# Soft combine on one NeuronCore: the maxima move from a TensorE product to a VectorE subtraction, the 1/Z weighing moves to GpSimd

## The reference

```python
def _L1_ffn_ref(x, phi_w, phi_b, expert_w, expert_b):
    logits = (jnp.einsum('tzd,ed->tze', x, phi_w) + phi_b).reshape(t, z, n, p)   # 64 experts x 32 slots
    D = jax.nn.softmax(logits, axis=3)
    C = jax.nn.softmax(logits, axis=2)
    X_tilde = jnp.einsum('tznp,tzd->npd', D, x)
    ...
    Y_tilde = jnp.einsum('npd,ndH->npH', X_tilde, expert_w) + expert_b[:, None, :]
    return jnp.einsum('tznp,npH->tzH', C, Y_tilde)
x = x + 0.5 * _L1_ffn_ref(_layernorm(x), ...)
```

## Time and profile before

| What | Value |
|---|---|
| median of 3 runs | 2346.54 us (2342.49 to 2348.29) |
| the profiled execution, its time | 2333.07 us |
| the profiled execution, its span | 2331.2 us |
| mean granted TensorE clock | 0.943 of full |
| combine of the first soft stage | about 1332 to 1606 us of the span |
| combine of the second soft stage | about 2056 to 2331 us, the end of the program |

### The profile page before, as it was taken

How to read it: one execution, slowest core, us unless ns; L and a number is a source line. 1 busy time by engine, 2 the same in 40 slices (tenths; PEclk the granted TensorE clock), 3 DMA queues, 4 the chain that set the end, 5 groups by cost and what they waited for, 6 DMA issues and landing times.

```text
span 2331.2 us, 23318 instructions
## 1 busy us (share of the span) xinstructions
PE 1947.9 (84%) x6378; PEld 958.2 (41%) x6400; DVE 1627.1 (70%) x2176; ACT 1034.7 (44%) x1548; POOL 1230.9 (53%) x775
## 2 busy tenths in 40 slices
PE   4099576888888717968999899997977999999998
PEld 3077422333333505753444344443333444444443
DVE  7133587999999822348999666674895999856554
ACT  2322286555555232225555453342444555463332
POOL 4645104999999473526999500001973999900000
PEclk9999796999999958989999999998988999999999
DMA  7122383555555022323000000002633000000000
GB/s 256 56 87 89 100 131 108 177 172 174 176 169 179 32 70 77 106 91 91 0 0 0 0 1 0 0 0 71 170 94 90 0 0 0 0 1 10 4 9 14
DMA packets 108594, 163.42 MB, mean 70 GB/s; under 512 B 11379, under 2 KB 74174, under 8 KB 108391
## 3 DMA queue, kind: packets, MB, share of 16 engines
q1 hardware_dynamic: 100326, 146.23, 21.5%
q0 software_dynamic: 8192, 16.30, 2.1%
HBM read 124.89 MB, written 38.15 MB: 70 GB/s over the span
## 4 chain that ended last, share of the span: by engine, by line
PE 53%; DVE 17%; issue 14%; POOL 11%; ACT 4%; DMA 1%; POOLq 0%; DVEq 0%; ACTq 0%; SPq 0%
PE ps L1904 10%; PE ps L1877 10%; PE ps L1636 5%; POOL arena L560 5%; PE ps L1833 5%; PE ps L1823 5%; PE ps L1646 5%; PE ps L1762 3%; DVE arena L1331 2%; POOL slot_inputs L506 2%; PE ps L1878 2%; POOL arena L539 1%; DVE arena L1497 1%; DVE stats L1055 1%; DVE stage L1080 1%
## 5 line engine op out<-in xcount | busy, mean ns | idle before, releaser
L568 POOL TENSOR_TENSOR arena<-arena 128x1024 f32<-128x1024 f32 x128 | 244.7, 1912 | 79.5 <-DVE arena L1384 74.0
L1823 PE MATMUL ps<-c_phiT,arena 128*128 128x512 f32 x512 | 266.8, 603 | 8.4 <-ACT arena L809 5.3
L1877 PE MATMUL ps<-XT,c_phiT 128*128 (+1 forms) x512 | 261.9, 593 | 0.9
L1833 PE MATMUL ps<-arena 128*128 128x512 f32 x512 | 241.2, 595 | 5.6 <-POOL arena L560 5.6
L560 POOL TENSOR_TENSOR arena<-arena 128x1024 f32<-128x1024 f32 x128 | 244.7, 1913 | 0.0
L534 POOL TENSOR_TENSOR arena<-XT,arena 128x1024 f32<-128x1024 f32 x86 | 170.0, 2000 | 140.3 <-DMA arena<-input_gates 140.3
L1904 PE MATMUL ps<-arena 128*128 128x512 f32 x512 | 226.2, 601 | 11.1 <-DVE arena L1450 11.1
L596 POOL TENSOR_TENSOR arena<-arena 128x1024 f32<-128x1024 f32 x32 | 63.6, 2000 | 310.4 <-DMA arena<-value_rows 310.3
L823 ACT ACTIVATE arena<-ps 128x1024 f32<-128x1024 f32 x128 | 131.0, 1024 | 214.7 <-PE ps L1824 214.7
L1450 DVE TENSOR_TENSOR arena<-arena 128x4096 f32<-128x4096 f32 x32 | 140.2, 4422 | 120.2 <-ACT arena L889 120.2
L882 ACT ACTIVATE arena<-ps,c_phi_bc 128x512 f32<-128x512 f32 x256 | 174.7, 687 | 90.7 <-PE ps L1878 82.8
(11 more groups left out here) (228 smaller groups left out, 3494.8 us busy)
## 6 DMA issues: line engine op xcount, KB each, us to landing
arena<-input_gates SPq DMA_DIRECT2D x128, 512.0 KB, 3.8
arena<-value_rows SPq DMA_DIRECT2D x32, 512.0 KB, 5.3
arena<-slot_inputs SPq DMA_DIRECT2D x32, 258.0 KB, 2.9
arena<-in_L_ffn_w SPq DMA_DIRECT2D x32, 256.0 KB, 3.3
arena<-token_outputs SPq DMA_DIRECT2D x16, 512.0 KB, 7.4
slot_inputs<-arena SPq DMA_DIRECT2D x1, 4128.0 KB, 13.4
slot_inputs<-zero SPq DMA_DIRECT2D x1, 4128.0 KB, 35.9
token_outputs<-arena SPq DMA_DIRECT2D x1, 4096.0 KB, 17.8
```

The source lines that it names most:

```text
L568: pool.tensor_tensor(Ed[:, r, :].rearrange("p (n q) -> p n q", q=PSLOT), Lc[:, r, :].rearrange("p (n q) -> p n q", q=PSLOT), over(mD[:, r, ...
L1823: pe.matmul(pbank(2 * h + c), xts[:, r // 2, :], phiT[:, at:at + CHUNK], start=True, stop=False)
L1833: ins = pe.matmul(pbank(4 + 2 * h + c), xns[:, r // 2, :], Dd[:, r, CHUNK * c:CHUNK * (c + 1)], start=start, stop=stop, skip_group_check=True)
L1877: pe.matmul(pbank(t % 4), phiT[:, P * t:P * (t + 1)], xt(b, c), start=True, stop=False)
```

## The change

Three things change in the combine.

1. TensorE no longer adds the maxima tile by tile. Once per chunk `spread_maxima` puts the negated maxima, spread over the 128 slots, into bank 5 (bank 2 for the first chunk), and ScalarE copies them to `mS` in SBUF (`copy_m`). VectorE adds `mS` to the logits, two slot tiles at a time, from PSUM to `Ec` (`shifted`); ScalarE takes the exponential in place, from SBUF to SBUF. TensorE may refill a pair of banks when VectorE has read it.
2. GpSimd multiplies `Ec` by `Rz` (`weigh`), in four parts of 4 slot tiles, for all chunks but the last of a stage, which VectorE weighs in four such parts.
3. VectorE's order changes: all 8 `shifted` of a chunk come before `ln_apply` and the tree of that chunk, and `residual(v-1)`, with `ln_statistics(v-1)` in the first stage, stands between the tree of chunk v and the first `shifted` of chunk v+1. In the first two chunks of a stage the tree of chunk 0 is interleaved with the `shifted` of chunk 1, and `total(0)` stands ahead of tile 12 of chunk 1, not of tile 9.

In the diff `weigh` is from GpSimd's stream, `exp_T` (activations) from ScalarE's, `shifted` and the loop with `tree` and `residual` from VectorE's, and the matmuls from TensorE's.

```diff
+                def weigh(v, c):
+                    hold(pool, sem("Rz"), v + 1)
+                    for g in range(4):
+                        part = Ec[c][:, 4 * g:4 * (g + 1), :]
+                        pool.tensor_tensor(part, part, Rz.unsqueeze(1).to_broadcast([P, 4, CHUNK]), ALU.mult).then_inc(sem("C"), 1)
+                weigh(first, 0)
+                with pool.Fori(0, CHUNKS // 2 - 1) as i:
+                    weigh(first + 2 * i + 1, 1)
+                    weigh(first + 2 * i + 2, 0)
...
-                        hold(act, sem("LT"), ST * v + t + 1)
-                        if t == 0 and not first:
-                            hold(act, sem("yT_ps"), v - 1)
-                        act.activation(Ec[c][:, t, :], pbank(t % 4), ACT.Exp, bias=phi_bc[:, t:t + 1])\
-                            .then_inc(sem("Ec"), 1)
+                        if t % 2 == 0:
+                            hold(act, sem("shifted"), ST // 2 * v + t // 2 + 1)
+                        act.activation(Ec[c][:, t, :], Ec[c][:, t, :], ACT.Exp, bias=phi_bc[:, t:t + 1]).then_inc(sem("Ec"), 1)
...
+                def shifted(v, c, j, first=False):
+                    dve.wait_ge(sem("LT"), ST // 2 * v + j + 1)
...
+                    dve.tensor_tensor(Ec[c][:, 2 * j:2 * (j + 1), :], ps[:, 2 * (j % 2):2 * (j % 2) + 2, :],
+                                      mS.unsqueeze(1).to_broadcast([P, 2, CHUNK]), ALU.add).then_inc(sem("shifted"), 1)
...
-                    for g in range(2):
-                        half = ec[:, 8 * g:8 * (g + 1), :]
-                        dve.tensor_tensor(half, half, Rz.unsqueeze(1).to_broadcast([P, ST // 2, CHUNK]), ALU.mult)\
-                            .then_inc(sem("C"), 1)
...
+                    for c in range(2):
+                        v = base + 2 * i + c
+                        for j in range(8):
+                            shifted(v, c, j)
+                        if s == 0:
+                            ln_apply(4, 2 * i - 2 + c, c)
+                        for j in range(5):
+                            tree(v, c, j)
+                        if c == 0:
+                            residual(v - 1, i - 1, 1)
+                        else:
+                            residual(v - 1, i, 0)
+                weigh(base + CHUNKS - 1, 1)
...
+                        if t % 2 == 0 and not (early and t < 4):
+                            pe.wait_ge(sem("shifted"), ST // 2 * v + t // 2 - 1)
+                        ins = pe.matmul(pbank(t % 4), phiT[:, P * t:P * (t + 1)], xt(b, c), start=True, stop=True)
+                        if t % 2 == 1:
+                            ins.then_inc(sem("LT"), 1)
-                        pe.matmul(pbank(t % 4), row128[:, :],
-                                  mCT[:, ds(b * TIME + CHUNK * c, CHUNK)], start=False, stop=True).then_inc(sem("LT"), 1)
...
                     for t in range(ST):
-                        if t % 8 == 0:
-                            pe.wait_ge(sem("C"), 2 * v + t // 8 + 1)
+                        if t % 4 == 0:
+                            pe.wait_ge(sem("C"), 4 * v + t // 4 + 1)
```

More of the change, by code:

```diff
@@ L866, in slots_tanh, with copy_m, exp_T @@
                     act.preload_act_table_set("natural_log_exp_and_others")
-                def exp_T(v, c, first, before=None, beside=None, at=0):
+                def copy_m(v, bank):
+                    hold(act, sem("maxima_ps"), v + 4 * s + 5)
+                    act.activation(mS, pbank(bank), ACT.Copy).then_inc(sem("maxima"), 1)
+                def exp_T(v, c, before=None, beside=None, at=0):
                     for t in range(ST):
@@ L1426, in soft, with tree, weigh @@
                                       slotB[:, 1024 * h:1024 * (h + 1)], ALU.mult).then_inc(sem("slot_n"), 1)
+                base = CHUNKS * s
+                def shifted(v, c, j, first=False):
+                    dve.wait_ge(sem("LT"), ST // 2 * v + j + 1)
+                    if j == 0:
+                        dve.wait_ge(sem("maxima"), v + 4 * s + 5)
+                        if not first:
+                            dve.wait_ge(sem("yT_ps"), v - 1)
+                    dve.tensor_tensor(Ec[c][:, 2 * j:2 * (j + 1), :], ps[:, 2 * (j % 2):2 * (j % 2) + 2, :],
+                                      mS.unsqueeze(1).to_broadcast([P, 2, CHUNK]), ALU.add).then_inc(sem("shifted"), 1)
+                def tree(v, c, j):
+                    ec = Ec[c]
+                    dst, lo, hi = ((t8[:, 0:4, :], ec[:, 0:4, :], ec[:, 4:8, :]), (t8[:, 4:8, :], ec[:, 8:12, :], ec[:, 12:16, :]),
+                                   (t4, t8[:, 0:4, :], t8[:, 4:8, :]), (t2, t4[:, 0:2, :], t4[:, 2:4, :]), (t1, t2[:, 0, :], t2[:, 1, :]))[j]
+                    if j < 2:
+                        dve.wait_ge(sem("Ec"), ST * v + 8 * (j + 1))
+                    else:
+                        dve.wait_ge(sem("tree"), 5 * v + j)
+                    if j == 4 and not below(v, 1):
+                        dve.wait_ge(sem("Z"), v)
+                    dve.tensor_tensor(dst, lo, hi, ALU.add).then_inc(sem("tree"), 1)
+                def weigh(v, c):
+                    dve.wait_ge(sem("Rz"), v + 1)
+                    for g in range(4):
+                        part = Ec[c][:, 4 * g:4 * (g + 1), :]
+                        dve.tensor_tensor(part, part, Rz.unsqueeze(1).to_broadcast([P, 4, CHUNK]), ALU.mult).then_inc(sem("C"), 1)
+                for j in range(8):
+                    shifted(base, 0, j, True)
                 for g in range(4):
```

94 lines of the change are left out of this document (48 added, 46 removed).

## The result

The changed kernel takes 2436.15 us (median of 4 runs, 2434.70 to 2437.39) against 2345.75 us (4 runs) for the kernel before: a ratio of 1.0386, with an interval of 1.0368 to 1.0404. It is 90.4 us slower; 2437 had been forecast. Its profiled execution took 2434.7 us, with a span of 2432.9 and a mean granted clock of 0.925.

The account below looks back on a forecast made before the run. The prediction took TensorE to bound both soft stages; 83 (first-stage turns) - 19 (second stage) + 29 (heads) - 1 (tails) = +92 us gave 2437 us, slower by 3.9%, range 2385 to 2462.

Parts of the forecast that it names:

- The turn of the first stage: Between chunks, VectorE's statistics wait for GpSimd, so TensorE waits 14.6 us: 6 x (11.4 + 2.5) = +83 us.
- the clock: TensorE's logits after its long wait run at a lowered clock: 2.5 us a chunk, bounds 0 and 3.4.
- the exclusion: A VectorE instruction with two SBUF inputs waits for the whole GpSimd multiplication under way, 3.8 us each.
- Which instructions are held: In the first stage's statistics, four two-input instructions wait, one for each of GpSimd's four multiplications.
- The second stage: With no statistics behind `residual`, no wait for GpSimd at the turn; TensorE's whole gain stays: 6 x -3.2 = -19 us.
- The heads: At each stage's start, combine(0) ends later, waiting for GpSimd's parts: 2 x 14.6 = +29 us, lower bound 7.8 each.
- The alternation: In the heads, GpSimd's four parts and the tree of chunk 1 take turns, 3.8 and 2.3 us.
- The tails: VectorE's first part of the last chunk is shorter, -2.1 us; statistics ahead cost +0.7 in the first stage; together -1.
- The weighing's duration: GpSimd's multiplication of 2048 elements, extrapolated from 512 and 1024: 3.82 us, 3.78 from start to start.
- The offset: The median of the runs stands 13.5 us above the profiled execution; the same was added to the forecast.
- Partial waits: Rival: at the first stage's turn only one to three of four small instructions are held; 2375 to 2415 us, chance 0.15.
- no exclusion: Rival: the small instructions slip through beside GpSimd: -15 us, 2331; chance 0.10 together with anything hiding the wait.

Follow-up runs that it names:

- experiment 1: Changed kernel, but in the first soft stage GpSimd starts weighing a chunk only after VectorE's statistics of the chunk before: 2330.69 us, ratio 0.9992 to the kernel before.
- experiment 2: Changed kernel with the first stage's statistics behind the chunk's eight `shifted`, ahead of its tree, and the layer norm applied behind the tree: 2316.55 us, ratio 0.9931.
- experiment 3: Changed kernel with the weighing in eight parts of 2 slot tiles instead of four of 4: 2383.65 us, ratio 1.0221 to the kernel before.
- experiment 9: Changed kernel with `Rz` 2 numbers (8 bytes) earlier in SBUF: 2464.41 us, ratio 1.0500 to the kernel before.
- experiment 5: Kernel before with only the weighing moved to GpSimd; TensorE still adds the maxima and ScalarE reads PSUM: 2355.50 us, ratio 1.0042.
- experiment 6: Changed kernel with VectorE weighing every chunk ahead of `residual` and GpSimd idle, so only the maxima moved: 2471.39 us, ratio 1.0536 to the kernel before.
- Experiment 7: Kernel of experiment 2 with each stage's first chunk weighed by VectorE, ahead of the tree of chunk 1: 2321.00 us, ratio 0.9895 to the kernel before.
- experiment 10: Kernel of experiment 7 with total(0) at tile 10 instead of 12 and one tree addition of chunk 0 one `shifted` earlier: 2327.09 us, ratio 0.9922.
- experiment 4: Changed kernel with an unused copy of the statistics behind `residual` in the second soft stage too: 2528.38 us, ratio 1.0837 to the kernel before.

## Why the prediction was right

- **The turn of the first stage.** The prediction let the held instructions through at 6.6, 10.4, 14.2 and 18.0 us after the end of combine(v-1); they ended at 6.8, 10.6, 14.3 and 18.1. TensorE waited 14.46 us where 14.6 stood, the clock cost 2.6 where 2.5 was taken, and the six turns cost +84.0 where +83 did. Experiments 1 and 2 show that the exclusion is the cause, 3 and 9 that its unit is one multiplication of GpSimd, 5 and 6 that it counts only through `shifted`.
- **Which instructions are held: this step was wrong.** The prediction named lines 1076, 1077, 1078 and 1080 and took the two `tensor_scalar` for free. Held were 1076, 1078, 1080 and 1082, and 1082 is a `tensor_scalar` with one SBUF tensor; lines 1077 and 1081, each directly behind a held one, slipped through in about 0.15 us. Two errors cancelled: the time came out because GpSimd had four parts, not because the prediction knew which four would wait. It also passed over line 1084 (1069 before), which has two SBUF inputs; with parts left over it is held as well (experiment 3). Experiment 3 shows what limits the number: the parts that GpSimd has left, then five.
- **The second stage.** -19.4 for -19, 29.1 to 29.3 us a chunk. The tree that meets GpSimd's last part takes 9.76 us instead of 8.80 and hides it, as the prediction's 17.5 and 26.3 had it.
- **The heads.** +13.4 each for 14.6. Both parts that the prediction named are there. The alternation made GpSimd's four parts 21.36 us for 15.13, 6.2 us (6.8 had been taken). The other 7.1 (7.8 in the prediction) are the later start: total(0) came 37.5 us after the first logits instead of 30.9, behind five `shifted` and the whole tree, and GpSimd began at 41.2, when before the change combine(0) itself could begin at 39.2. Experiment 7 takes the alternation away and gains only 3.2 us of the 6.2 in the first head, since VectorE starts the product 3.8 us later than GpSimd did. No run took the later start away; experiment 10 was meant to and left total(0) where it was.
- **The tails.** +0.8 and -2.0 for +0.7 and -2.1.
- **The weighing's duration.** 3.81 us, with 3.78 from start to start, for 3.82 and 3.78. The extrapolation from 1090 and 2000 ns held, but only for this placement: with `Rz` 8 bytes earlier it would have been 0.7 us off and the total 25 us higher. The estimate of 4.3 us from the Trainium skill, GPSIMD Engine Reference, section 2.1, lies between the two measured times, 3.81 and 4.5.
- **The offset.** The prediction added 13.5 us for the median over the profiled execution. The profiled execution of the kernel before is like those on the chip of experiments 1 to 4: there 13 executions of it took 2331.16 to 2334.44 us, and the first combine began 1331.0 to 1333.2 us into the span (1332.4 in the kernel before's profile), where in the profiles of the other experiments it began at 1342.4 to 1347.1. So the offset lies ahead of the combines. Since all terms were differences within the combines, adding them to the median was right; the prediction had no row that showed it.
- **Small slips in the sums.** The turn of the kernel before adds up to 32.6, not 32.7. VectorE's small instructions end at 18.0 + 0.6 = 18.6, not 18.8; the first `shifted` began at 18.6. The tree of chunk 0 ends at 1355.4 + 6.0 + 8.8 = 1370.2, not 1370.5. None matters for the total.
- **The rivals.** Partial waits (2380 to 2404) and no exclusion (2331) are excluded by the timeline of after. Without the exclusion at the turn the kernel comes out at 0.9992 (experiment 1), so the faster side was near, one wait away.

## What to carry to other kernels

Before work goes to GpSimd, list what VectorE does in the same stretch with its tensors in SBUF, however small, and what is queued behind it: a 128 x 4 instruction can cost as much as the longest GpSimd instruction under way. If somebody waits for that queue, move the small instructions to a stretch in which GpSimd is idle, or let GpSimd start after them; a start 2.8 us later won back 3.9% here. And when a resource is taken off the path in two steps (the logits' maxima, the weighing), ask who empties the buffers afterwards: moving the maxima made VectorE's every delay TensorE's, which it had not been before.

## What the runs showed of the hardware

- VectorE's `tensor_scalar` with one SBUF input waits for GpSimd as well: 3.78 us for 128 x 4 numbers (line 1082), and 2.96 instead of 1.11 us for four of 128 x 128 in experiment 1. The Trainium skill, SBUF — State Buffer, section Who interferes with whom, lists instructions in a two-port performance mode beside those with two SBUF inputs; whether these were in one, the trace doesn't show.
- An instruction directly behind a held one can slip through before GpSimd's next: 0.15 us for lines 1077 and 1081 each time. In the attention stage line 1062, at the same position, was held; what decides it stayed open.
- A GpSimd multiplication of 128 x 2048 with a broadcast operand took 3.81 or 4.52 us, depending on 8 bytes in the place of that operand (experiment 9). Why is open.
- After a wait of 14.46 us TensorE ran at 1.2 GHz for about 5 us; after waits of 11.75 and 7.81 us in experiment 6 its 24 instructions took 13.12 and 13.64 us. The price differs between turns with nearly the same wait: 12.18 to 13.60 us after some 14.5 us in the changed kernel, 12.18 to 13.64 after 7.8 to 8.1 us in the second stage of experiment 6. In these runs the shorter wait was not the cheaper one.
